# Loads, splits and turns of a vision tower's first stages in another order, with the memory term made per group inside the attention loop

## The reference

```
h = patches @ W_proj.T + b_proj + pos_emb        # 36 patches of 768 per image
h = concat(cls_tok, h)                           # (16, 37, 256)
x = layernorm(h)
q, k, v = x @ Wq.T, x @ Wk.T, x @ Wv.T           # per head
attn = softmax(where(causal, q k^T, min)) @ v
sq = elu(q) + 1
A_mem = (sq @ mem) / (sq @ z + 1e-6)             # mem (4, 64, 64), z (4, 64, 1)
g = sigmoid(betas)
h = h + (g * A_mem + (1 - g) * attn) @ Wo.T + bo
x = layernorm(layernorm(h)) * gamma + beta
logits = x @ router_w.T                          # 8 experts, the best 2 per token
# each expert takes the first 185 of its tokens, in token order
h = h + sum over kept (token, expert): p * w3[e] (silu(w1[e] x) * (w2[e] x))
```

## Time and profile before

| | us |
|---|---|
| median of 3 runs (249.26, 249.62, 251.57) | 249.62 |
| the profiled execution's own time | 249.06 |
| its span, first to last instruction | 247.3 |
| PE busy in the span | 210.5 |
| DVE, ACT, POOL busy | 88.7, 76.2, 54.9 |
| mean granted clock of TensorE | 0.912 |

### The profile page before, as it was taken

The page is one execution under the profiler, slowest core; times in us unless marked ns, Lnnn a source line. Parts: engine busy times, 40 slices in busy tenths (PEclk is TensorE's granted clock), DMA queues, the critical chain, the costliest instruction groups (busy, mean ns, idle before and its releaser), DMA issues.

```text
span 247.3 us, 3565 instructions
## 1 busy us (share of the span) xinstructions
PE 210.5 (85%) x1307; PEld 187.7 (76%) x1307; DVE 88.7 (36%) x279; ACT 76.2 (31%) x224; POOL 54.9 (22%) x55
## 2 busy tenths in 40 slices
PE   0185956989998785989999999999999999999970
PEld 0185956965766454459999999999999999999970
DVE  6849874443678654203211111111111111111120
ACT  2433311634554114023622232322222323222220
POOL 0245343000004446300004004022040040220404
PEclk9999995995579855599999999999999999999997
DMA  7935995520001322167429058095290580410211
GB/s 247 337 117 127 322 351 233 215 98 1 0 21 41 97 61 65 51 170 238 199 62 447 2 212 314 0 358 184 70 439 10 223 305 0 170 12 0 23 9 17
DMA packets 10299, 36.15 MB, mean 146 GB/s; under 512 B 3328, under 2 KB 6738, under 8 KB 7978
## 3 DMA queue, kind: packets, MB, share of 16 engines
q1 hardware_dynamic: 7514, 31.90, 35.7%
q0 software_dynamic: 2336, 2.13, 4.4%
q10 hardware_dynamic: 432, 1.90, 2.0%
HBM read 31.42 MB, written 5.35 MB: 149 GB/s over the span
## 4 chain that ended last, share of the span: by engine, by line
PE 74%; DVE 8%; DMA 5%; issue 4%; POOL 4%; ACT 2%; POOLq 1%; SPq 0%
PE bank L538 33%; PE bank L550 16%; DMA x_flat<-in 5%; PE bank L582 3%; PE bank L522 3%; DVE hn L793 3%; PE bank L469 2%; POOL token_rows L1027 2%; PE bank L424 2%; POOL rstd L1014 1%; PE bank L437 1%; PE bank L563 1%; PE bank L388 1%; PE bank L449 1%; PE bank L390 1%
## 5 line engine op out<-in xcount | busy, mean ns | idle before, releaser
L538 PE MATMUL bank<-xb,w 128*128 128x185 f32 x512 | 91.5, 322 | 1.1 <-ACT xb L710 1.1
L538 PEld LDWEIGHTS bank<-xb,w 128*128 128x128 f32 x512 | 81.9, 190 | 1.6 <-issue 1.2
L977 DVE TENSOR_TENSOR hid<-bank,sg 128x185 f32<-128x185 f32 x64 | 22.5, 351 | 113.4 <-ACT sg L722 113.4
L550 PE MATMUL bank<-hid,w 128*128 128x185 f32 x256 | 50.2, 319 | 0.0
L1044 POOL DMA_INDIRECT out<-yw,slot_token x16 | 23.8, 1489 | 118.3 <-ACT yw L742 109.1
L722 ACT ACTIVATE sg<-bank 128x185 f32<-128x185 f32 x64 | 20.9, 326 | 89.2 <-PE bank L538 89.2
L550 PEld LDWEIGHTS bank<-hid,w 128*128 128x128 f32 x256 | 42.1, 189 | 0.0
L337 PE MATMUL bank<-wp_hi,x_hi 128*111 128x256 f32 x36 | 11.2, 310 | 12.3 <-DVE x_lo L799 12.3
L337 PEld LDWEIGHTS bank<-wp_hi,x_hi 128*111 128x111 f32 x36 | 7.0, 194 | 12.5 <-issue 12.5
L1027 POOL DMA_INDIRECT token_rows<-rowbuf,dest x12 | 11.6, 968 | 13.4 <-DVE dest L936 11.6
L1035 POOL TENSOR_TENSOR rstd<-var,minus_half 111x1 f32<-111x1 f32 (+1 forms) x6 | 3.4, 571 | 34.3 <-DVE var L908 34.2
(11 more groups left out here) (145 smaller groups left out, 265.9 us busy)
## 6 DMA issues: line engine op xcount, KB each, us to landing
w<-in SPq DMA_DIRECT2D x8, 2048.0 KB, 10.6
w<-in SPq DMA_DIRECT2D x8, 1024.0 KB, 4.8
x_flat<-in SPq DMA_DIRECT2D x6, 333.0 KB, 10.7
token_rows<-rows_in SPq DMA_DIRECT2D x1, 1728.0 KB
rows_in<-token_rows SPq DMA_DIRECT2D x8, 144.0 KB
w_sb<-in ACTq DMA_DIRECT2D x1, 1024.0 KB, 8.6
wp_sb<-in ACTq DMA_DIRECT2D x1, 768.0 KB, 5.5
out<-h SPq DMA_DIRECT2D x5, 111.0 KB
```

The lines of the kernel that those rows point to most:

```text
L538: mm = pe.matmul(o, w[:, part, k, :], xb[b][:, k, :], start=(k == 0), stop=(k == KD - 1))
L550: mm = pe.matmul(bank[YT_BANK[k]][:, 0:NS], w3[e % 2][:, fc, k * P:(k + 1) * P], hid[:, step % 4, :], start=(fc == 0), stop=(fc == FC - 1))
L977: dve.tensor_tensor(hid[:, step % 4, :], bank[GU_BANK[step % len(GU_BANK)]][:, NS:2 * NS], sg[:, step % 2, :], ALU.mult).then_inc(hid_done, 1)
```

## The change

Loads: `wp_sb` comes in two halves with a semaphore each; `w_sb` moves from ACT's queue to SP's, behind the second group of `x`. Splits: both halves of `wp_lo` and all three `w_lo` move from POOL to DVE; POOL clears `rowbuf` in place of DVE. PE runs two multiplications on `wp_sb` while it waits. `turn_hn` and `value` go one group later, and the q tiles of the first half of the tokens are made before the last values. `bo` is no longer added to `h` by POOL but by one more matmul, of a single row, in `project`. The memory term's stretch goes: `mem_bd` is multiplied by the gate once, and per group PE makes 111 x 256 of it (`remember`), DVE multiplies by 1/den (`weigh_memory`), and `attend` first clears the bank with a zero product, adds the turned memory rows with two multiplications by `ident`, and then the attention. The copy of the sum out of PSUM goes from DVE's `add_memory` to ACT's `copy_ao`.

```diff
@@ SP
                 if g == 0:
                     sp.dma_start(pos[:, :], pos_cls).then_inc(in_pos, 16)
                     sp.dma_start(bias[:, :], bias_rows).then_inc(in_pos, 16)
+                if g == 1:
+                    sp.dma_start(w_sb[:, :, :, :], wqkvoT).then_inc(in_w, 16)
...
@@ PE
-            for t in range(GROUPS + 2):
+            def keep_warm(passes):
+                pe.wait_ge(in_wp[0], 16)
+                for n in range(passes):
+                    pe.matmul(bank[7][:, :], wp_sb[:, 0, 0:P], wp_sb[:, 0:2, :].rearrange("p k d -> p (k d)"), start=True, stop=True)
...
+            keep_warm(2)
+            for t in range(GROUPS + 3):
                 if t < GROUPS:
                     embed(t)
-                if 1 <= t <= GROUPS:
-                    turn_hn(t - 1)
-                if t >= 2:
-                    value(t - 2)
+                if t == GROUPS + 1:
+                    pe.wait_ge(w_hi_done, 2)
+                    pe.wait_ge(w_lo_done, 2)
+                    for n in range(2):
+                        project_in(0, n)
+                if 2 <= t <= GROUPS + 1:
+                    turn_hn(t - 2)
+                if t >= 3:
+                    value(t - 3)
...
-            def memory_turn():
...
-            def memory():
...
+            def remember(g):
+                R = ROWS[g]
+                if g == 0:
+                    pe.wait_ge(mem_gated, 1)
+                else:
+                    pe.wait_ge(ao_done, g)
+                for m in range(2):
+                    mm = pe.matmul(bank[PV_BANK][0:R, MEM_AT + m * P:MEM_AT + (m + 1) * P], sqT[:, m, cols(g)], mem_bd[:, m, :],
+                                   start=True, stop=True)
+                mm.then_inc(mem_in_psum, 1)
...
             def attend(g):
                 R = ROWS[g]
+                pe.wait_ge(mem_done, g + 1)
+                pe.matmul(bank[PV_BANK][:, 0:2 * R], zero_bf[:, 0:P], zero_bf[:, 0:2 * R], start=True, stop=False, skip_group_check=True)
+                for m in range(2):
+                    pe.matmul(bank[PV_BANK][:, m * R:(m + 1) * R], mem_rows[0:R, g % 2, 2 * m:2 * m + 2, :].rearrange("p h c -> p (h c)"),
+                              ident[0:R, 0:R], start=False, stop=False, skip_group_check=True)
                 pe.wait_ge(pT_done, g + 1)
...
             def project(g):
...
+                pe.matmul(bank[WO_BANK][0:R, 0:D], ones_row[:, 0:R], bo_row[:, :], start=True, stop=False)
...
-            memory_den()
             pe.wait_ge(k_done, 4)
             pe.wait_ge(mask_set, 1)
             score(0)
             score(1)
-            memory_turn()
-            memory()
+            memory_den()
             for t in range(GROUPS + 7):
-                for lag, stage in ((6, route), (3, turn_probs), (4, project), (6, count), (5, turn_xn), (0, score), (3, attend)):
+                for lag, stage in ((6, route), (3, turn_probs), (4, project), (3, remember), (6, count), (5, turn_xn), (0, score), (3, attend)):
...
@@ ACT
+            def copy_ao(g):
+                R = ROWS[g]
+                act.wait_ge(pv_done, g + 1)
+                if g >= 2:
+                    act.wait_ge(wo_done, g - 1)
+                act.activation(aoT[:, g % 2, :, 0:R], bank[PV_BANK][:, 0:2 * R].rearrange("p (m c) -> p m c", m=2),
+                               ACT.Copy).then_inc(ao_done, 1)
...
-                for lag, stage in ((1, softmax), (5, copy_xnT), (2, copy_probsT)):
+                for lag, stage in ((4, copy_ao), (1, softmax), (5, copy_xnT), (2, copy_probsT)):
...
@@ DVE
+            def weigh_memory(g):
+                R = ROWS[g]
+                dve.wait_ge(mem_in_psum, g + 1)
+                if g >= 2:
+                    dve.wait_ge(pv_done, g - 1)
+                dve.tensor_tensor(mem_rows[0:R, g % 2, :, :], bank[PV_BANK][0:R, MEM_AT:MEM_AT + D].rearrange("p (h c) -> p h c", h=HEADS),
+                                  den[0:R, g, :].unsqueeze(2).broadcast_to([R, HEADS, HD]), ALU.mult).then_inc(mem_done, 1)
...
-                for lag, stage in ((5, residual), (4, add_memory), (1, row_max), (6, rank), (5, norm2), (6, send), (2, normalise)):
+                for lag, stage in ((5, residual), (1, row_max), (3, weigh_memory), (6, rank), (5, norm2), (6, send), (2, normalise)):
...
@@ POOL
             for g in range(GROUPS):
                 R = ROWS[g]
-                if g < 3:
-                    pool.wait_ge(w_hi_done, g + 1)
-                    which = (2, 0, 1)[g]
-                    pool.tensor_tensor(w_lo[:, which, :, :], w_sb[:, which, :, :], w_hi[:, which, :, :].bitcast(F32),
-                                       ALU.subtract).then_inc(w_lo_done, 1)
                 pool.wait_ge(var1_done, g + 1)
...
-            for g in range(GROUPS):
-                R = ROWS[g]
-                pool.wait_ge(hn_done, g + 1)
-                pool.tensor_tensor(h[0:R, g, :], h[0:R, g, :], bo_b[0:R, :], ALU.add).then_inc(h_bo_done, 1)
```

More of the change, by code:

```diff
@@ L163, in vit_tower @@
         yw = [[sb(f"yw{b}_{s}", [P, D]) for s in range(2)] for b in range(2)]
-        in_embed = sem("in_embed")
+        in_wp = [sem(f"in_wp{n}") for n in range(2)]
         in_x = [sem(f"in_x{g}") for g in range(GROUPS)]
@@ L254, in cols @@
             return slice(g * G_ROWS, g * G_ROWS + ROWS[g])
-        WIDE = [(m, n) for m in range(2) for n in range(2)]
+        WIDE = [(m, n) for n in range(2) for m in range(2)]
+        QK_BANK = (6, 7, 0, 1)
+        WP_HALVES = (slice(0, KE // 2), slice(KE // 2, KE))
         def half(n):
@@ L367, in value, with project_in @@
                 mm.then_inc(v_in_psum, 1)
-            for t in range(GROUPS + 2):
+            def keep_warm(passes):
+                pe.wait_ge(in_wp[0], 16)
+                for n in range(passes):
+                    pe.matmul(bank[7][:, :], wp_sb[:, 0, 0:P], wp_sb[:, 0:2, :].rearrange("p k d -> p (k d)"), start=True, stop=True)
+            def project_in(which, n):
+                m, hf = WIDE[n]
+                o, rows = bank[QK_BANK[n]][:, 0:HALF], slice(m * P, (m + 1) * P)
+                if which == 1:
+                    pe.wait_ge(q_done, n + 1)
+                for k in range(KD):
+                    pe.matmul(o, w_hi[:, which, k, rows], hnT_hi[:, k, half(hf)], start=(k == 0), stop=False)
+                    pe.matmul(o, w_hi[:, which, k, rows], hnT_lo[:, k, half(hf)], start=False, stop=False)
+                    mm = pe.matmul(o, w_lo[:, which, k, rows], hnT_hi[:, k, half(hf)], start=False, stop=(k == KD - 1))
+                mm.then_inc(qk_in_psum, 1)
@@ L393, in memory_den @@
+            pe.wait_ge(h_copied, GROUPS)
+            for n in range(2, len(WIDE)):
+                project_in(0, n)
+            pe.wait_ge(w_hi_done, 3)
+            pe.wait_ge(w_lo_done, 3)
+            for n in range(len(WIDE)):
+                project_in(1, n)
             def memory_den():
@@ L626, in split_x @@
                 act.activation(x_hi[g % 2], x_sb[:, g, :, :], ACT.Copy).then_inc(x_hi_done, 1)
-            act.wait_ge(in_embed, 16)
-            for n in range(2):
-                ks = slice(n * KE // 2, (n + 1) * KE // 2)
-                act.activation(wp_hi[:, ks, :], wp_sb[:, ks, :], ACT.Copy).then_inc(wp_hi_done, 1)
-            split_x(0)
-            act.wait_ge(in_w, 16)
-            for which in (2, 0, 1):
-                act.activation(w_hi[:, which, :, :], w_sb[:, which, :, :], ACT.Copy).then_inc(w_hi_done, 1)
-                if which == 2:
-                    split_x(1)
@@ L639, in _, with split_wp, split_w @@
-            for t in range(GROUPS + 2):
+            def split_wp(n):
+                act.wait_ge(in_wp[n], 16)
+                act.activation(wp_hi[:, WP_HALVES[n], :], wp_sb[:, WP_HALVES[n], :], ACT.Copy).then_inc(wp_hi_done, 1)
+            def split_w(which):
+                if which == 2:
+                    act.wait_ge(in_w, 16)
+                act.activation(w_hi[:, which, :, :], w_sb[:, which, :, :], ACT.Copy).then_inc(w_hi_done, 1)
+            split_wp(0)
+            split_x(0)
@@ L1064, in _constants @@
     token = (np.minimum(q[:, None] + G_ROWS * np.arange(GROUPS)[None, :], T) - FAR).astype(np.float32)
[L1065 to L1068 removed]
+    return [mask, before, np.eye(P, dtype=np.float32), token, expert, AREA * expert[None, :]]
 def kernel(x, cls_tok, L0_tok_W_proj, L0_tok_b_proj, L0_tok_pos_emb, L0_attn_Wq, L0_attn_Wk, L0_attn_Wv, L0_attn_Wo,
```

201 lines of the change are left out of this document (84 added, 117 removed).

## The result

The changed kernel takes 265.5 us (median of 4 executions, 262.5 to 267.3) against 249.4 for the kernel before: ratio 1.0585, 95% interval 1.047 to 1.070. The forecast was 256, with 252 to 261 for its own case and 246 to 267 as the whole range. The direction was right and the time lies inside the whole range, but outside the forecast's own; the loss is 16 us where 7 were forecast.

What follows compares the result with a forecast made beforehand. PE's chain was taken to bound the kernel, with a ring of routing stages, no engine full, in the attention loop. -8.5 - 5.0 + 20.5 = +7.0 on 249.06 gave 256 us, 8-in-10 range 246 to 267.

Steps and rivals of the forecast that it cites:

- its own case: Whole kernel with the loop's clock mixed as before: 256 us, range 252 to 261, chance 0.46.
- Stretch A: Start to end of the q and k tiles (49.13): earlier loads and a shorter last norm, -8.5 us.
- Stretch B: From memory_den's start (49.13) to the first turn_probs (62.43): memory stages removed, 13.3 to 8.3, -5.0 us.
- Stretch C: Attention loop, first turn_probs (62.43) to last count (99.2), 36.8 us: added PE work and waits, +20.5 us.
- the waits: In the loop, PE waits for ACT 1.0 five times (5.0) and for DVE 1.4 in three steps (4.2).
- the PE work: Products added per loop group: 1.55 us at full clock or 2.7 at half, 8.2 or 14.3 in all.
- Half of the old steps ran at either clock; I take +20.5: Attention loop: grows by 17 at full clock, 23 at half; with the old clock mix, +20.5 us.
- Rival 2: Loop stays at half clock because PE's gaps leave it unpacked: loop +31.7, sum +20.7, 270 us; chance 0.20.
- The rule on idle gaps: Only longer idle gaps drop the clock, so the loop keeps full clock: sum -3.3, 245.8 us; chance 0.20.
- Rival 3: Loop's added waits overlap existing ones, only PE work counts: 246.6 to 250 us, within 1%; chance 0.14.

Runs made afterwards that it cites:

- both orders moved: Changed kernel with copy_ao ahead of copy_probsT on ACT and rank ahead of weigh_memory on DVE; 254.6 us over 12 executions, 259.4 over all 25.
- wide products: Changed kernel, its engine orders kept, with the product of bo and the zero product over 128 rows instead of one; 259.4 us, ratio 1.034.
- the early part alone: Kernel before with only the change's early order of loads, splits, turns and q and k tiles, bo added by POOL after the last v tile; 244.8 us, ratio 0.976.

## Why the forecast was right in its parts and wrong in its sum

**Stretch A, right.** `x` of group 1 landed at 11.87 (forecast 11.7), embedding 2 started at 17.02 (17.2), the last norm took 0.40 (0.41), the q and k tiles ended at 40.5 (40.6). `w_lo` and `wp_lo` on DVE cost nothing that shows in these landmarks.

**Stretch B, the gain was forecast 1.9 too small.** I priced what is left of it at 6.8 with full clock and 10.8 with half and took 8.3; it had a mean clock of 0.94 and took 6.4.

**Stretch C, the waits were right in kind and a little large.** PE's idle time ahead of the product of `bo`, released by ACT L726, was four times 0.87 or 0.88 and once 0.62: 4.1 where 5.0 was forecast. `count`'s waits for DVE were 1.04 in the step shown and 0.94 and 1.23 in the two beside it: 3.2 against 4.2. Undoing them one at a time gave 4.9 and 4.1 us at the medians, on another chip.

**Stretch C, the PE work was priced too low at half clock.** Forecast 2.7 a group; measured from start to start 1.12 for the product of `bo` (forecast 0.86), 0.86 for `remember` (0.86), 1.13 for the turned memory rows (0.75), 0.29 for the zero product (0.25): 3.4. I also counted the last group, of 37 rows, as a third, but its product of `bo` took 0.99 and its turned rows 0.99, nearly as much as a full group's. From start to start the additions of all six groups come to 18.3 us in this execution, some of them at full clock, where I had 14.3 for half clock throughout.

**The step that failed: "Half of the old steps ran at either clock; I take +20.5".** I let the new loop have the old loop's mix of clocks, and said that the number would fail there first. It had full clock for about 7 of its 68 us, where the old one had some 14 of 36.8 by its mean clock of 0.69 (I had read 15.7, and called that half). Rival 2 (chance 0.20) priced C at half clock throughout at +31.7, and measured is +31.5. That agreement is partly luck, closer than its parts: its work was 4.0 too low and its waits 1.9 too high. Its reason was at best half of it. I gave "gaps of 1.0 and 1.4 in each step"; the gaps went in the kernel with both orders moved, PE was busy 4.00 of 4.00 us and the clock stayed down all the same. What the runs put in its place is the kind of work that the change adds: with the products of `bo` and of zeros over one row 25 executions have a median of 259.4, over 128 rows six have 243.1. The waits have a share too, since in the changed kernel, which has them, the wide products give only 6 us.

How the 16 us divide can be read off twice. The changed kernel's shortest execution has a half-clock time of 61 us (span 260.7, clock 0.883) and takes 262.5; the line through the 48 executions of the kernel before is at 254.8 there (251.6 at 50 us, 0.29 for each more): 8 apart. And with wide products the change costs 8.7. So some 8 us are work and waits, near the 7.0 forecast for them at the old mix, and the other 8 or 9 are 30 us more at the lower clock, at 0.29. This division is an estimate: the line's own executions reach from 37 to 60 us, and with the 0.44 of the kernel with both orders moved the clock's share would be 13.

**The rule on idle gaps.** The prediction weighed the Trainium skill's "TensorE: Matmul & The Clock Gate", section "Why this matters for your kernels", by which the clock drops in mid-kernel through idle gaps between bursts, and gave it 0.20. These runs don't agree with it as the only cause: the clock was low through 16 us in which the profile shows no idle PE ahead of a matmul, and the longest wait in the changed kernel's loop was 0.88 us.

**Rival 3** (the additions hide) is out: each added wait and product can be seen in the timeline, the loop grew by more than their sum (31.5 against 18.3 and 7.3), and each wait went when its entry was moved.

**Open.** Why one execution of a kernel gets 42 us of half clock and the next 78 was not tried; nor which of the other thin products weigh (the scores use 64 rows at a time). That widening raises the clock is shown for the two products together and, across chips, for that of `bo` alone; what exactly the chip adds up is not. One rival stands untested: the narrow product also delays the weight loads beside it and takes 0.27 us more, so the pause beside it, and not the rows it leaves empty, could be what counts. A narrow product with the loads kept in place, or a wide one with a pause, would tell them apart.

## What to carry to other kernels

When TensorE's clock moves between its levels inside a loop, price the loop at both levels and treat the level as an outcome of the edit, not as a constant of the place; the span and mean clock of several executions separate the two effects. Don't add a bias with a one-row product in such a loop: let an idle engine add it, or spread the same product over all 128 rows. And a stage moved into a ring should be put in each engine's list so that nobody's next wait stands behind it: two table entries and one add moved to POOL turned a loss of 16 us into a gain of 11 to 12.

## What the runs showed of the hardware that I had not expected

- A product over one row is not cheaper than one over 128 and can be dearer: 1.12 against 0.85 us, start to start, float32, 256 columns, half clock.
- PE busy for 16 us at the lower clock level, with no idle time ahead of any matmul in the profile.
- One kernel in 25 executions between 248.4 and 264.0 us, in step with its mean clock (0.915 to 0.851).
- POOL's six adds of `bo` took about the same wherever they stood: 5.0 us and, with the early part alone, 4.3 beside the q and k tiles, 4.5 in the loop. Beside the tiles PE waited 0.41 and 1.12 for ACT's copy of q, a wait that the kernels without them there don't show.
